# Graph network, first loop: products of message scalars and edge directions on VectorE, one instruction a step, in place of 24 on ScalarE

## The chip, the cores and the metric

The kernel runs on one core of one Trainium2 chip. The metric is the device time of one execution in microseconds (us); a version's time is the median of its runs. The engines are TensorE (PE; its weight loads are shown apart as PEld), VectorE (DVE), ScalarE (ACT), GpSimd (POOL) and SyncE (SP). They run side by side and wait for one another by semaphores only.

## What is computed

Two layers of a graph network over 6250 nodes with 128 features and 106250 directed edges sorted by their target. Only the first is touched. Its edge part, cut to what matters:

```python
Y1 = SQ3 * edge_vec / |edge_vec|                 # 3 numbers per edge
w = (silu(silu(emb @ w0 + b0) @ w1 + b1) @ w2 + b2).reshape(-1, 4, 32)
ss, vv = xs[senders], xv[senders]                # 32 scalars, 32 x 3 vectors of the source node
m0 = w[:, 0] * ss
m1 = w[:, 1][:, :, None] * ss[:, :, None] * Y1[:, None, :]
m2 = w[:, 2][:, :, None] * vv
m3 = w[:, 3] * (einsum('emc,ec->em', vv, Y1) / SQ3)
msg = segment_sum over receivers of (m0, m3), (m1, m2)
```

The node part behind it (two small products, a residual, a layer norm) and the second layer, with its own loop over the edges, stay as they are. The change is about `m1`.

## The kernel before

The edges lie in tiles of 128 (edges on the partitions). A step of the first loop takes 8 tiles; there are 104 steps, written as 26 iterations of 4 steps (`SLOTS`), most of them in hardware loops. `edges0` writes one program for each engine. A step, numbered j, uses one of two sets of buffers (h = j % 2) and one of four buffers for gathered rows (u = j % 4). By engine, in the order of its program:

- **GpSimd** issues 8 indirect DMAs a step (`gather_step`, L731), each fetching 128 node rows into `gx`. Ahead of a step's gathers it waits for the list of indices (L744), for `used` (L746: the buffer was read) and, from iteration 17 on, for TensorE's second MLP product, `h2_mm` (L749), which paces it.
- **SyncE** loads the list of indices for the next iteration (L888) once the gathers of this slot have landed, and `emb` (L892) once TensorE has done its first product `h1_mm`; both stand in one queue, with the loads and stores of the node part between them.
- **TensorE** keeps the MLP three steps ahead. In step j: 8 products of the one-hot matrix with the first half of the message columns into `ps_a` (L1105, waits for `half_ok`), the third MLP product, which makes the weights of step j + 1 in `ps_w` (L785, L787, signals `w_mm`), the second MLP product (L197, waits for `h1_ok`, signals `h2_mm`), 8 products with the other half of the columns (L1105, waits for `plain_ok` and `y_ok`, signals `sum_mm`), and the first MLP product for a later step (L1101, waits for `h2_ok`, signals `h1_mm`). Products of the node part (L1111, L1117, L1118, L1130) stand between these.
- **VectorE** makes the message columns: L808 `vy` = vectors times directions; L805 `ws` = weights times scalars (waits for `w_mm`, signals `ws_ok`); L811 and L814 the first half (`m0`, `m2`; signals `half_ok`); L818, L818, L821 the dot product and `m3` (signals `plain_ok`); between them L1259 adds the sums of the step before from `ps_a` to the node sums at a start position that is read into a register (L1255, TENSOR_LOAD). L1250 makes the next one-hot matrix. A part of the node work follows in each step.
- **ScalarE** does the silu of the first and of the second product (L192), and makes `m1` = `ws` times direction in `by_component` (L829): for each of the 8 tiles and each of the 3 components one activation of 128 x 32 with the direction as its scale for each partition, 24 a step, 12 ahead of the first silu and 12 behind it, then `y_ok`. Copies of the node part (L1018, L1023, L1033, L1039) and, once an iteration, two table loads (L1063, L1066) stand between.

`ws`, `y`, `vy`, `gx` and `msg` lie in SBUF, `ps_w` and `ps_a` in PSUM. The last steps are unrolled; there VectorE makes `m1` itself, by `all_components` (L824), since they are handled in parts.

Of the kernel before, what the change touches and what calls it, by code (L numbers as in the profile page):

```python
# [31 lines left out]
TPS = 8  # L32
PPS = TPS // 2
SLOTS = 4
# [26 lines left out]
LOOPS = STEPS // SLOTS  # L61
# [783 lines left out]
def edges0(nc, a, k, dram, w, later, v, mlp, left):  # L845

    with ExitStack() as ctx:
# [12 lines left out]
        gate = gate_x = k["gate"]  # L860
        used, half_ok, plain_ok, ws_ok, y_ok, own, sum_mm, acc_own = (
            m.sem(n) for n in ("used", "half_ok", "plain_ok", "ws_ok", "y_ok", "own0", "sum_mm", "acc_own"))
        later_ld, iota_ok, w_ok, w_own, sums_ok = (m.sem(n) for n in ("later_ld", "iota_ok", "w_ok", "w_own0",
# [19 lines left out]
        with nc.Block(no_gpsimd_drain=True) as block:  # L883
# [115 lines left out]
            def _(e):  # L999
                def components(j, h, tiles):  # L1000
                    for t in tiles:
                        last = msgs[h].by_component(e, t, w["y"][:, bass.ds(j * TPS + t, 1), :]
                                                    .rearrange("p t c -> p (t c)"))
                    return last

                CLEAR = (T * NACC - v["end"]) // (LAG * SLOTS)
# [34 lines left out]
                def steps(i, unit, before, last=False):  # L1041
                    for u in range(SLOTS):
                        j, h = i * SLOTS + u, u % 2
                        if not last or u < SLOTS - 2:
                            e.wait_ge(ws_ok, j + 1)
                            components(j, h, range(0, TPS // 2))
                            layer0_silu(e, w, mlp, 1, j + 3)
                            components(j, h, range(TPS // 2, TPS)).then_inc(y_ok, 1)
                        if before and u == 0:
                            table_out(i - (LAG + 1), 1)  # L1050
                        if unit and u == 2:
                            nodes_t(i - LAG)
                        if unit and u == 3 and not last:
                            table_out(i - LAG, 0)
                        if not last or u < SLOTS - 2:
                            layer0_silu(e, w, mlp, 2, j + 3)
                        if not unit:
                            clear_high(j)
                        if unit and u == 0:
                            copy_sums(i - LAG, i * SLOTS)  # L1060
                        if unit and u == 1:
                            clear_sums(i - LAG)
                            e.preload_act_table(ACT.Sqrt)  # L1063
                            root(i - (LAG - 1), slice(0, UB))
                            if not last:
                                e.preload_act_table(ACT.Silu)  # L1066
# [31 lines left out]
            def _(e):  # L1098
# [68 lines left out]
                def steps(i, unit, before, last=False):  # L1167
                    for u in range(SLOTS - 1 if last else SLOTS):
# [19 lines left out]
                        e.wait_ge(plain_ok, j + 2)  # L1188
                        if not last or u < SLOTS - 2:
                            e.wait_ge(y_ok, j + 1)  # L1190
                        sums(h, 1).then_inc(sum_mm, 1)
# [54 lines left out]
            def _(e):  # L1246
# [124 lines left out]

                def messages(i, u, first=False, unit=False, before=False, whole=False, counted=False):

# [9 lines left out]
                    mine.w2_product(e, wt, vec).then_inc(half_ok, 1)  # L1383
                    if whole:
                        e.wait_ge(ws_ok, j + 1)
                        mine.all_components(e, y)
                    e.wait_ge(own, j * 3 + 1)
# [57 lines left out]
                for u in range(SLOTS - 1):  # L1445
                    messages(LOOPS - 1, u, unit=True, before=True, whole=u == SLOTS - 2)
                last_first(0)
# [1148 lines left out]
```

## Time and profile before

| | us |
|---|---|
| median of 3 runs | 2890.57 (2885.65 to 2907.28) |
| profiled execution, its own time | 2876.12 |
| span of the profiled execution | 2874.2 |
| busy in the span: PE / DVE | 2014.0 / 1473.3 |
| busy in the span: ACT / POOL | 1329.9 / 1601.4 |
| ScalarE's L829, 2448 instructions | 539.8 |

The profile is of one execution. An instruction's row has its start, its duration, engine, line, what it writes and reads, and in brackets the idle time of its engine just before it with what ended that. "issue" is idle time that nothing in the profile ended; "remote" is a releaser that the profile does not name. DVE starts an instruction while the one before still writes, so that starts lie closer than durations. The first loop lies between about 60 and 1494 us.

### The profile page before, as it was taken

Reading aid. Unit: us, or ns where it says so; the run is one execution under the profiler, and the core shown is the slowest. Engines: PE = TensorE matmul, PEld = TensorE weight load, DVE = VectorE, ACT = ScalarE, POOL = GpSimd, SP = SyncE. Lnnn points to the kernel's source line nnn. Section 1 sums busy time; section 2 is a strip of 40 time slices with the busy share of each in tenths; the row PEclk is TensorE's granted clock in tenths of the full one; section 3 lists DMA queues with packets and bytes.
Section 4 is the critical chain, followed back from the end, with each engine's and each line's share of the span. In section 5 each row is a group of like instructions: output and inputs, shape, how many; then the busy total and the mean of one; then the engine's idle time right before and its main releaser. Section 6 shows DMA issues by size and latency. Waiting matters only on the chain. (4 is left out here: it accounts for less than half of the span.)

```text
span 2874.2 us, 43625 instructions
## 1 busy us (share of the span) xinstructions
PE 2014.0 (70%) x10027; PEld 1570.4 (55%) x10027; DVE 1473.3 (51%) x3718; ACT 1329.9 (46%) x4378; POOL 1601.4 (56%) x1680
## 2 busy tenths in 40 slices
PE   6777678768777787878785766565666566566656
PEld 4555455545554565656563655554665555555555
DVE  6443344334343444444453445665666666666666
ACT  5545456445464565555542333434343334334333
POOL 6655454555544555656546555566666666665662
PEclk7778788878787888889897787787777767767778
DMA  8311112111121121222125553333333333333331
GB/s 266 91 38 45 49 53 63 55 54 49 50 63 50 53 59 57 60 60 65 52 81 164 154 143 88 96 94 91 91 97 94 93 91 92 97 85 95 94 94 49
DMA packets 221613, 238.23 MB, mean 83 GB/s; under 512 B 73212, under 2 KB 163240, under 8 KB 221131
## 3 DMA queue, kind: packets, MB, share of 16 engines
q0 software_dynamic: 53472, 110.50, 14.8%
q1 hardware_dynamic: 79835, 71.35, 8.1%
q10 hardware_dynamic: 88256, 55.83, 7.4%
q8 instruction: 16, 0.26, 0.0%
q14 instruction: 34, 0.28, 0.0%
HBM read 191.88 MB, written 45.62 MB: 83 GB/s over the span
## 5 line engine op out<-in xcount | busy, mean ns | idle before, releaser
L731 POOL DMA_INDIRECT gx<-node_d,idx x815 | 789.2, 968 | 647.8 <-issue 279.1
L731 POOL DMA_INDIRECT gp<-p_tab_d,idx x831 | 789.0, 949 | 555.8 <-issue 272.1
L1105 PEld LDWEIGHTS ps_a<-hot,msg 128*128 128x128 f32 x3324 | 469.4, 220 | 315.8 <-issue 294.2
L1105 PE MATMUL ps_a<-hot,msg 128*128 128x128 f32 x3324 | 506.0, 310 | 153.9 <-issue 80.4
L829 ACT ACTIVATE msg<-ws,y 128x32 f32<-128x32 f32 x2448 | 539.8, 310 | 5.6 <-issue 3.1
L2140 PE MATMUL ps_e<-win,hot_x 128*128 128x129 f32 x1664 | 328.9, 365 | 289.3 <-issue 181.8
L2140 PEld LDWEIGHTS ps_e<-win,hot_x 128*128 128x128 f32 x1664 | 298.6, 271 | 314.7 <-issue 211.0
L805 DVE TENSOR_TENSOR ws<-ps_w,gx 128x256 f32<-128x256 f32 (+1 forms) x105 | 44.2, 421 | 521.6 <-remote 386.5
L192 ACT ACTIVATE h<-ps_h,b 128x512 f32<-128x512 f32 x208 | 141.8, 682 | 332.8 <-remote 198.0
L2277 DVE TENSOR_TENSOR hot_x<-key_row,ps_s 128x1024 f32<-128x1024 bf16 x104 | 126.4, 1216 | 323.7 <-remote 299.4
L2025 ACT ACTIVATE hid<-hid,score 128x128 f32<-128x128 f32 x832 | 277.5, 392 | 10.1
L2229 PE MATMUL ps_g<-hot,hid 128*128 128x128 f32 x1664 | 237.8, 294 | 43.1 <-issue 41.6
L2229 PEld LDWEIGHTS ps_g<-hot,hid 128*128 128x128 f32 x1664 | 228.3, 209 | 60.4 <-issue 51.4
L787 PE MATMUL ps_w<-w,h 128*128 128x256 f32 x832 | 246.2, 444 | 11.0 <-issue 10.7
L787 PEld LDWEIGHTS ps_w<-w,h 128*128 128x128 f32 x832 | 172.1, 217 | 90.6 <-issue 67.0
L2021 ACT ACTIVATE score<-hid 128x3 f32<-128x3 f32 (+1 forms) x312 | 60.6, 194 | 272.9 <-DVE hid L2322 181.7
L2322 DVE TENSOR_TENSOR hid<-ps_e,gp 128x387 f32<-128x387 f32 (+1 forms) x312 | 142.0, 509 | 73.8 <-remote 66.2
L1259 DVE TENSOR_TENSOR acc<-acc,ps_a 128x256 f32 x105 | 44.3, 422 | 264.3 <-remote 189.1
L1101 PE MATMUL ps_h<-emb,w 16*128 16x512 f32 x202 | 136.8, 762 | 38.9 <-ACT h L192 29.5
L2299 DVE TENSOR_TENSOR acc<-acc,ps_g 128x128 f32 x416 | 119.4, 287 | 25.8 <-issue 12.1
L2235 PE MATMUL ps_s<-hot_n,sc 128*128 128x128 f32 x416 | 76.4, 310 | 79.2 <-issue 59.6
L1039 ACT ACTIVATE acc<-ps_x 128x258 f32<-128x258 f32 x44 | 16.9, 384 | 247.0 <-remote 196.9
(304 smaller groups left out, 2556.7 us busy)
## 6 DMA issues: line engine op xcount, KB each, us to landing
win<-q_tab_d ACTq DMA_DIRECT2D x408, 64.5 KB
key_row<-key_row_d ACTq DMA_DIRECT2D x100, 256.0 KB
gp<-p_tab_d,idx POOLq DMA_INDIRECT x831
gx<-node_d,idx POOLq DMA_INDIRECT x815
p_tab_d<-acc SPq DMA_DIRECT2D x23, 516.0 KB
q_tab_d<-unit_area SPq DMA_DIRECT2D x36, 258.0 KB
q_tab_d<-acc SPq DMA_DIRECT2D x5, 774.0 KB, 4.0
emb<-emb_d SPq DMA_DIRECT2D x102, 32.0 KB
```

The lines of the kernel that those rows point to most:

```text
L192: e.activation(mlp[f"h{layer}"][:], mlp["ps_h"][:], ACT.Silu, bias=w[f"b{layer - 1}"][:]).then_inc(ok, 1)
L731: e.indirect_dma_start(out=buf[:, h, t, :], out_offset=None, in_=table, in_offset=bass.IndirectOffsetOnAxis(ap=idx[:, h, t:t + 1], axis=0) ...
L787: last = e.matmul(ps_w[:, 2 * t:2 * t + 2, :], h2[:, t * P:(t + 1) * P], w["w2"][:], start=False, stop=t % 2 == 1)
L829: last = e.activation(self.cols[1][:, tile, c, :], self.ws[:, tile, :], ACT.Copy, scale=y[:, c:c + 1])
L1101: e.matmul(ps_h[:], w["w0"][:], emb[:, h, :], start=True, stop=True).then_inc(h1_mm, 1)
L1105: last = e.matmul(ps_a[:, h, b, :], msgs[h].tile(t, b), hot[:, h, t, :], start=t == tiles.start, stop=t == tiles.stop - 1)
L2025: last = e.activation(hid[:, h, t, 0:H], hid[:, h, t, 0:H], ACT.Relu, scale=score[:, h, t:t + 1])
L2140: last = e.matmul(ps_e[:, q, at:at + PW], hot_x[:, h, t, :], win[:, h, t // 2, :], start=True, stop=True)
L2229: e.matmul(ps_g[:, h, t // 2, :], hid[:, h, t, 0:H], hot[:, h, t, :], start=t % 2 == 0, stop=t % 2 == 1)
L2277: e.tensor_tensor(hot_x[:, h].rearrange("p t n -> p (t n)"), key_row[:, h, :], part.to_broadcast([P, TPS * P]), ALU.is_equal).then_inc(hx_ ...
L2299: e.tensor_tensor(at, at, ps_g[:, h, p, :].rearrange("p (t n) -> p t n", t=T), ALU.add)\
L2322: e.tensor_tensor(hid[:, h, mine, :], ps_e[:, q, 0:n * PW].rearrange("p (t n) -> p t n", t=n), gp[:, u, mine, :], ALU.add).then_inc(pre_ok, 1)
```

## The change

The 24 activations a step go away, with the semaphore `y_ok` and TensorE's wait for it. VectorE calls `all_components` in every step, between the first half of the columns and the dot product: one product of `ws` (repeated over 3 components) with `y` (repeated over 32 columns), 128 x 768, both operands in SBUF. It waits for VectorE's own `ws_ok`.

```diff
@@ block.scalar
-                def components(j, h, tiles):
-                    for t in tiles:
-                        last = msgs[h].by_component(e, t, w["y"][:, bass.ds(j * TPS + t, 1), :]
-                                                    .rearrange("p t c -> p (t c)"))
-                    return last
...
                         if not last or u < SLOTS - 2:
-                            e.wait_ge(ws_ok, j + 1)
-                            components(j, h, range(0, TPS // 2))
                             layer0_silu(e, w, mlp, 1, j + 3)
-                            components(j, h, range(TPS // 2, TPS)).then_inc(y_ok, 1)
@@ block.tensor
                         e.wait_ge(plain_ok, j + 2)
-                        if not last or u < SLOTS - 2:
-                            e.wait_ge(y_ok, j + 1)
                         sums(h, 1).then_inc(sum_mm, 1)
@@ block.vector, messages
                     mine.w2_product(e, wt, vec).then_inc(half_ok, 1)
-                    if whole:
-                        e.wait_ge(ws_ok, j + 1)
-                        mine.all_components(e, y)
+                    e.wait_ge(ws_ok, j + 1)
+                    mine.all_components(e, y)
                     e.wait_ge(own, j * 3 + 1)
                     mine.dot_sum(e, 1).then_inc(own, 1)
```

How the order on the engines changes. Line numbers of the changed kernel are lower by 9 on TensorE's L1105 (now L1096), by 6 on ScalarE's copies and by 11 on VectorE's lines from L1250 on.

VectorE, one step in the looped part, before:

```order
L808 TENSOR_TENSOR vy<-gx,y 128x768 [waits landed0]
L805 TENSOR_TENSOR ws<-ps_w,gx 128x256 [waits w_mm]
L811 TENSOR_TENSOR msg<-ps_w,gx 128x8x32
L814 TENSOR_TENSOR msg<-ps_w,gx 128x8x96
L818 TENSOR_TENSOR vy<-vy 128x8x32 [waits own0]
L1255 TENSOR_LOAD start [waits half_ok]
L1259 ISA [waits acc_own,sum_mm]
L1259 TENSOR_TENSOR acc<-acc,ps_a 128x2x128
```

and now:

```order
L808 TENSOR_TENSOR vy<-gx,y 128x768 [waits landed0]
L805 TENSOR_TENSOR ws<-ps_w,gx 128x256 [waits w_mm]
L811 TENSOR_TENSOR msg<-ps_w,gx 128x8x32
L814 TENSOR_TENSOR msg<-ps_w,gx 128x8x96
L824 TENSOR_TENSOR msg<-ws,y 128x8x96 [waits ws_ok]
L818 TENSOR_TENSOR vy<-vy 128x8x32 [waits own0]
L1244 TENSOR_LOAD start [waits half_ok]
L1248 ISA [waits acc_own,sum_mm]
L1248 TENSOR_TENSOR acc<-acc,ps_a 128x2x128
```

L824 has come between L814 and L818; the rest keeps its order, and the register load still waits for `half_ok` alone.

ScalarE, a step of an iteration that has the table loads behind it, before:

```order
L829 ACTIVATE msg<-ws,y 128x32 [waits ws_ok]
L829 ACTIVATE msg<-ws,y 128x32 x11
L192 ACTIVATE h<-ps_h,b 128x512 [waits h1_mm]
L829 ACTIVATE msg<-ws,y 128x32 x12
L192 ACTIVATE h<-ps_h,b 128x512 [waits h2_mm]
L1023 ACTIVATE acc<-zero 128x2x256 [waits sums_ok0]
L1063 ACT_TABLE_LOAD
L1028 ACTIVATE rstd<-rstd 128x2 [waits var_ok_0]
```

and now:

```order
L192 ACTIVATE h<-ps_h,b 128x512 [waits h1_mm]
L192 ACTIVATE h<-ps_h,b 128x512 [waits h2_mm]
L1017 ACTIVATE acc<-zero 128x2x256 [waits sums_ok0]
L1054 ACT_TABLE_LOAD
L1022 ACTIVATE rstd<-rstd 128x2 [waits var_ok_0]
```

Both silus and the copies stay in their order; the wait for `ws_ok` has left this engine.

TensorE, end of a step, before:

```order
L197 MATMUL ps_h<-h,w 128x512 [waits h1_ok]
L1105 MATMUL ps_a<-hot,msg 128x128 [waits y_ok,plain_ok]
L1105 MATMUL ps_a<-hot,msg 128x128 x7
L1101 MATMUL ps_h<-emb,w 128x512 [waits emb_in0,h2_ok]
L1105 MATMUL ps_a<-hot,msg 128x128 [waits acc_own,half_ok]
```

and now:

```order
L197 MATMUL ps_h<-h,w 128x512 [waits h1_ok]
L1096 MATMUL ps_a<-hot,msg 128x128 [waits plain_ok]
L1096 MATMUL ps_a<-hot,msg 128x128 x7
L1092 MATMUL ps_h<-emb,w 128x512 [waits emb_in0,h2_ok]
L1096 MATMUL ps_a<-hot,msg 128x128 [waits acc_own,half_ok]
```

Nothing moves here; one of two waits is gone.

## Rows read from the trace of the kernel before

**Rows 1.** busy us by stretch: start:end, length, PE, PEld, DVE, ACT, POOL, PE clock
```profile
60.00:1016.00 956.00, 719.97 (x3302) 503.79 (x3303) 400.03 (x790) 499.98 (x1838) 491.36 (x509) 0.80 0.19 55
1016.00:1494.00 478.00, 396.23 (x1900) 282.86 (x1899) 216.63 (x446) 274.84 (x1012) 274.94 (x287) 0.87 0.21 62
```

**Rows 2.** groups by line, 60 to 1494 us; busy, mean ns, idle before
```profile
L731 POOL DMA_INDIRECT gx<-node_d,idx x793 | 765.1, 965 | 639.6 <-issue 272.7 <-DMA idx<-in_src 209.1 <-PE ps_h L197 77.5
...
L829 ACT ACTIVATE msg<-ws,y 128x32 f32<-128x32 f32 x2448 | 539.8, 310 | 5.6 <-issue 3.1 <-DVE ws L805 2.2
...
L805 DVE TENSOR_TENSOR ws<-ps_w,gx 128x256 f32<-128x256 f32 (+1 forms) x105 | 44.2, 421 | 521.6 <-remote 386.5 <-PE ps_w L787 97.5 <-issue 37.5
...
L1259 DVE TENSOR_TENSOR acc<-acc,ps_a 128x256 f32 x103 | 43.5, 422 | 263.8 <-remote 189.1 <-PE ps_a L1105 38.2 <-issue 36.5
```

**Rows 3.** waits of GpSimd, 60 to 1016 us; total, times, longest
```profile
POOL gx L731 <- DMA idx<-in_src: 209.1, 29, 12.4
```

**Rows 4.** waits of GpSimd, 1016 to 1494 us
```profile
POOL gx L731 <- PE ps_h L197: 77.5, 13, 18.9
POOL gx L731 <- remote: 50.7, 20, 2.7
```

**Rows 5.** waits of TensorE, 60 to 1494 us
```profile
PE ps_a L1105 <- remote: 41.1, 11, 8.3
...
PE ps_a L1105 <- ACT msg L829: 21.6, 17, 2.4
```

**Rows 6.** order of time, one step about 1178 us: start, duration, engine, line
```profile
1178.43 1.99 PE L787 MATMUL ps_w<-w,h 128*128 128x256 f32 x8
...
1180.34 2.64 ACT L829 ACTIVATE msg<-ws,y 128x32 f32<-128x32 f32 x12
...
1182.69 0.94 POOL L731 DMA_INDIRECT gx<-node_d,idx  x1 [0.30 <-issue]
...
1185.44 3.16 PE L1105 MATMUL ps_a<-hot,msg 128*128 128x128 f32 x16 [3.82 <-remote]
1185.49 0.42 DVE L805 TENSOR_TENSOR ws<-ps_w,gx 128x256 f32<-128x256 f32 x1 [6.50 <-remote]
1185.63 0.38 ACT L1033 ACTIVATE acc<-ps_x 128x256 f32<-128x256 f32 x1 [2.65 <-remote]
...
1195.09 0.94 POOL L731 DMA_INDIRECT gx<-node_d,idx  x1 [0.30 <-issue]
...
1195.67 1.02 PE L197 MATMUL ps_h<-h,w 128*128 128x512 f32 x2
...
1197.88 0.42 DVE L805 TENSOR_TENSOR ws<-ps_w,gx 128x256 f32<-128x256 f32 x1 [5.56 <-remote]
...
1198.72 0.94 POOL L731 DMA_INDIRECT gx<-node_d,idx  x1 [2.70 <-PE ps_h L197]
```

**Rows 7.** order of time, VectorE without the whole product at 1198 us
```profile
1198.55 0.95 DVE L814 TENSOR_TENSOR msg<-ps_w,gx 128x768 f32<-128x768 f32 x1
...
1200.35 0.42 DVE L1259 TENSOR_TENSOR acc<-acc,ps_a 128x256 f32 x1 [0.52 <-issue]
```

**Rows 8.** order of time, VectorE with it, second last step
```profile
1484.09 0.95 DVE L814 TENSOR_TENSOR msg<-ps_w,gx 128x768 f32<-128x768 f32 x1
...
1484.95 0.95 DVE L824 TENSOR_TENSOR msg<-ws,y 128x768 f32<-128x768 f32 x1
...
1486.15 0.41 DVE L1259 TENSOR_TENSOR acc<-acc,ps_a 128x256 f32 x1
```

**Rows 9.** order of time, a gather that starts beside L808
```profile
1085.24 0.95 DVE L808 TENSOR_TENSOR vy<-gx,y 128x768 f32<-128x768 f32 x1
1085.37 1.64 POOL L731 DMA_INDIRECT gx<-node_d,idx  x1 [0.30 <-issue]
```

**Rows 10.** TensorE waits for L829, first of six
```profile
365.99 1.24 PE L1105 MATMUL ps_a<-hot,msg 128*128 128x128 f32 x9 [1.16 <-ACT msg L829]
```

**Rows 11.** TensorE waits for L829, last of the six
```profile
946.46 1.80 PE L1105 MATMUL ps_a<-hot,msg 128*128 128x128 f32 x14 [0.67 <-ACT msg L829]
```

More of the change, by code:

```diff
@@ L860, in edges0 @@
         gate = gate_x = k["gate"]
-        used, half_ok, plain_ok, ws_ok, y_ok, own, sum_mm, acc_own = (
-            m.sem(n) for n in ("used", "half_ok", "plain_ok", "ws_ok", "y_ok", "own0", "sum_mm", "acc_own"))
+        used, half_ok, plain_ok, ws_ok, own, sum_mm, acc_own = (
+            m.sem(n) for n in ("used", "half_ok", "plain_ok", "ws_ok", "own0", "sum_mm", "acc_own"))
         later_ld, iota_ok, w_ok, w_own, sums_ok = (m.sem(n) for n in ("later_ld", "iota_ok", "w_ok", "w_own0",
@@ L1042, in steps @@
                     for u in range(SLOTS):
-                        j, h = i * SLOTS + u, u % 2
+                        j = i * SLOTS + u
                         if not last or u < SLOTS - 2:
-                            e.wait_ge(ws_ok, j + 1)
-                            components(j, h, range(0, TPS // 2))
                             layer0_silu(e, w, mlp, 1, j + 3)
-                            components(j, h, range(TPS // 2, TPS)).then_inc(y_ok, 1)
                         if before and u == 0:
@@ L1370, in last_second, with messages @@
                     mine.w3_product(e, wt).then_inc(plain_ok, 1)
-                def messages(i, u, first=False, unit=False, before=False, whole=False, counted=False):
+                def messages(i, u, first=False, unit=False, before=False, counted=False):
                     j, h = i * SLOTS + u, u % 2
@@ L1445, in _ @@
                 for u in range(SLOTS - 1):
-                    messages(LOOPS - 1, u, unit=True, before=True, whole=u == SLOTS - 2)
+                    messages(LOOPS - 1, u, unit=True, before=True)
                 last_first(0)
```

## The prediction

> **What bounds the kernel now.** I looked first at busy time by stretch. In the first loop (60 to 1494 us, 104 steps) no engine is full: TensorE 720 of 956 us and then 396 of 478, ScalarE 500 and 275, VectorE 400 and 217, GpSimd 491 and 275 [rows 1]. The loop is held by waits between engines. Then I read the groups by line. VectorE stands idle 521.6 us before L805, so it is the least loaded of the engines in the chain; ScalarE's L829 takes 539.8 us in 2448 instructions and has almost no idle time before it [rows 2]. That looks like a bound, but who waits for it? TensorE is stopped at L1105 by L829 for 21.6 us in 17 waits, and for 41.1 us in 11 waits with an unnamed releaser [rows 5], 62.7 us together. That is the largest sum that taking L829 away can set free directly.
>
> Next the waits of GpSimd, which issues eight gathers a step. To 1016 us it waits 209.1 us in 29 waits for lists of indices [rows 3]; SyncE loads them behind a wait for TensorE's first MLP product. After 1016 us it waits for the second MLP product, 77.5 us in 13 and 50.7 us in 20 waits [rows 4]. Busy and waiting together fill the loop on this engine.
>
> The order of time shows why. TensorE's last weight product (L787) ends at 1178.43 + 1.99 = 1180.42, and VectorE, idle, starts L805 only at 1185.49. The last gather of the batch ends at 1182.69 + 0.94 = 1183.63. The same happens a step later: the batch's last gather ends at 1195.09 + 0.94 = 1196.03, VectorE starts at 1197.88, and the second product, over at 1195.67 + 1.02 = 1196.69, lets GpSimd go on at 1198.72 [rows 6]. So what is signalled in the later part of a batch of gathers reaches the others about 1.85 us after its last gather. From one L805 at 1185.49 to the next at 1197.88 is one period: 12.39 us, of which 9.70 are eight gathers of 0.95 with 0.30 between them, 1.85 this delay, and 0.84 GpSimd's start behind the signal (1198.72 - 1197.88). In the second stretch this period, not ScalarE's work, sets most steps.
>
> **The change part by part.** ScalarE loses L829: 539.8 us of its 774.8 in the loop. Only the start of its other work moves, and TensorE loses the wait for y_ok.
>
> (a) *The waits of TensorE.* Of the 17 short waits, six lie where GpSimd has no batch running: the first ends at 365.99 and cost 1.16 us, the last at 946.46 with 0.67 [rows 10, 11]; the others cost 0.25, 1.87, 1.22 and 1.51, all six 6.7 us. There TensorE's progress is what GpSimd's next indices wait for, so I count them in full: -6.7. The others fall in a batch, whose end is not TensorE's to move: 0, with a bound of 21.6 - 6.7 = 14.9 us of gain.
>
> (b) *The waits of the second kind.* In the second stretch one step in four has one like that of 3.82 us at 1185.44: ScalarE ended L829 at 1180.34 + 2.64 = 1182.98, within the batch, and TensorE saw it after the batch [rows 6]. Without it these 16 products run at once. But TensorE's next work waits for ScalarE's copy, which is released only after the batch and ends at 1185.63 + 0.38 = 1186.01, where these products now end at 1188.60; so TensorE gains at most 2.6 us, not 3.8, and some 2.4 with the start of a matmul. Its second product would end at 1194.3 in place of 1196.69; GpSimd still sees it about 1.7 to 1.85 us after 1196.03, near 1197.8 in place of 1197.9 or so. The gain is 0.2 us in each of 9 iterations: -1.8. Bounds: 0, and -41.1 if all of it comes back.
>
> (c) *VectorE's new instruction.* L824 already stands in the second last step: 0.95 us, and the next instruction starts 0.86 after it. Over 102 steps that is 88 us of VectorE's time. How much lies on its chain? Without it, L814 starts at 1198.55 and the sum L1259 at 1200.35, after 0.52 us of idle time that nobody released [rows 7]: the engine is reading the start position into a register there. With it, L814 starts at 1484.09 and L1259 at 1486.15 [rows 8]. That is 2.06 in place of 1.80 us: the new instruction fills the gap and costs 0.26 us, not 0.86. All 36.5 us of such idle time before L1259 [rows 2] are cover. What is queued behind L824 is the dot product, the sum and L821; TensorE needs L821's result only behind a third and a second product, 1.99 and 1.02 us [rows 6]. The first half of the message columns (L814, half_ok) goes ahead of L824 and isn't late. With 521.6 us idle before L805 I cost this 0. If the cover is gone (steps where L805 follows L808 at once), it costs 0.26 to 0.86 us each; the upper bound is 88 us.
>
> (d) *GpSimd beside it.* A gather takes 0.95 us, but one that starts 0.13 us after L808 took 1.64 and so ended at 1087.01, where L808 ended at 1086.19 [rows 9]: 0.69 us longer. L808 reads both operands from SBUF. L814 reads one from PSUM, and the gather that starts at 1198.72, 0.17 us after it, takes 0.94 [rows 6, 7]. L824 reads both from SBUF. The Trainium skill says so too (SBUF — State Buffer, "Who interferes with whom"): a VectorE instruction with two SBUF inputs contends with a GpSimd instruction that reads SBUF, and the later one waits. The same section infers that such a product does not hold up the making of descriptors; by that this part would cost nothing, by the row it costs, and the row decides.
> Size: 793 gathers at 965 ns [rows 2] against 950 are 11.9 us too much. The operations with two SBUF inputs are now L808 (0.95) and two L818 (0.84 us) a step, 183 us in 102 steps, so 0.065 us of delay per us, and 0.062 us for one L824. But in the second stretch the two are in step. GpSimd's first gather starts 0.84 us after L805, its second 0.95 + 0.30 later, at 2.09 [rows 6]. L824 would start 1.53 and end 2.48 us after L805's start (1197.88 to 1198.55 is 0.67 [rows 6, 7], then 0.86 [rows 8]). The second gather starts inside it and waits for its end, less the 0.13 us that the pair of rows 9 leaves uncounted (0.82 to the end, 0.69 of delay): 0.26 us. About 27 of the 36 steps there have this order (rows 4 count 33 waits, a few of them much longer): 27 x 0.26 = +7.0. The other 66 steps at 0.062: +4.1. Bounds: 0, and 0.69 x 102 = 70 us.
>
> **Sum.** -6.7 - 1.8 + 0 + 7.0 + 4.1 = +2.6 us. The profiled execution took 2876.1 us (span 2874.2), so 2879; it lies 14.5 us below the median of 2890.6, so the forecast for a median is 2893 us. A measurement of this kernel can tell about 1%, 29 us, from no change; this is no change.
>
> **The rivals.**
> *TensorE's waits come back whole.* For it: 62.7 us are really waited, ScalarE is freed of 540 us, and TensorE is the busiest engine. Against: in batches the partners' releases come after the last gather anyway. Then -62.7 + 11.1 = -52, 2839 us.
> *The second product gets through before the batch ends.* If TensorE, ahead by some us, signals in the early part of a batch, GpSimd runs on without the 1.7 us: 27 x 1.7 = 46 us less. Against: the weight product that ended at 1180.42 did so 3.2 us before the batch's end and still came 5 us late [rows 6], and the gain of 2.4 us is small beside a batch of 9.7. -46 - 8.5 + 11.1 = -43, 2847 us.
> *The gathers are lengthened in every step* (the slower side). Place: the gather that starts beside L824, on the engine whose period sets the step. If each step meets it with about 0.5 us, between the 0.26 worked out and the 0.69 seen, it is +51 - 8.5 = +43, 2933 us. From (28.9 + 8.5) / 102 = 0.37 us a step on it is slower by over 1%. For it: both engines are released by the same signal, so they meet systematically. Against: VectorE is released when GpSimd pauses, and in the first stretch that pause for indices is 7.2 us on average (209.1 / 29), so that L824 is over before the gathers begin.
> *VectorE becomes the bound*: +88 us, 2978. Against: 521.6 us idle.
> That the change doesn't do what it says I rule out: in its order every ScalarE product is gone and L824 stands once in each step.
>
> **How the numbers follow.** Forecast's case 0.52, the first rival 0.17, the second 0.08, the third 0.18, the fourth 0.05. Faster by over 1%: 0.25; within 1%: 0.52; slower: 0.23. The steps of this loop are irregular, and any shift regroups batches; the likeliest case's own range is 2868 to 2915. With the rivals I give 2845 to 2930, which leaves out the fourth and the far ends of the first and third.
>
> **What would show it.** Right: ScalarE's busy time falls by some 540 us and VectorE's rises by some 90, while the loop still ends near 1494 us; GpSimd's waits in the second stretch keep their 2.5 us; L731's mean rises from 965 to about 980 ns, with second gathers of 1.2 us; idle time before L1259 by "issue" nearly vanishes. Wrong: TensorE's idle time in the loop falls by 50 us and the span with it (first rival); periods of GpSimd under 12 us (second); L731 near 1000 ns or more and a longer loop (third); idle time before L805 gone (fourth).

## The result and the profile after

The changed kernel took 2803.18 us (median of 4 runs, 2793.11 to 2817.75), the kernel before 2888.11 us beside it. The ratio is 0.9695, 95% interval [0.9639, 0.9751]: faster by 3%. The forecast was 2893 us with a range of 2845 to 2930. Two later comparisons gave 0.9815 [0.9742, 0.9888] and 0.9735 [0.9688, 0.9781].

One thing must be known to read the numbers: the experiments came to several chips, and these are of two kinds. On some the kernel before takes 2868 to 2922 us, as in the first comparison; on two others it takes 2162 and 2164 us. They are called slower and quicker chips here; two of the slower ones were used twice and were slow both times. Ratios are always to the kernel before on the same chip.

The head of the page of the changed kernel, profiled at 2817.75 us (the slowest of its four runs):

```profile
span 2815.9 us, 38846 instructions
PE 1998.1 (71%) x10027; PEld 1548.5 (55%) x10027; DVE 1563.1 (56%) x3820; ACT 818.1 (29%) x1930; POOL 1632.6 (58%) x1680
```

The span is 58.3 us shorter (before 2874.2). ScalarE is busy 511.8 us less (L829 alone was 539.8; what is left in the loop takes 263.9 in place of 235.0), VectorE 89.8 more; GpSimd, whose program nobody touched, 31.2 more. The groups of the first loop, 60 to 1494 us, against [rows 2]:

```profile
L731 POOL DMA_INDIRECT gx<-node_d,idx x792 | 796.7, 1006 | 549.6 <-issue 238.8 <-DMA idx<-in_src 173.1 <-PE ps_h L197 80.8
...
L824 DVE TENSOR_TENSOR msg<-ws,y 128x768 f32<-128x768 f32 (+1 forms) x105 | 98.9, 942 | 0.0
L1248 DVE TENSOR_TENSOR acc<-acc,ps_a 128x256 f32 x105 | 44.1, 420 | 288.0 <-remote 240.0 <-PE ps_a L1096 26.3 <-issue 20.8
L805 DVE TENSOR_TENSOR ws<-ps_w,gx 128x256 f32<-128x256 f32 (+1 forms) x105 | 44.1, 420 | 340.6 <-remote 232.6 <-PE ps_w L787 71.4 <-issue 36.5
```

The last gather of the loop ends at 1414.2 us, before at 1482.3: the loop is 68 us shorter, and the rest of the program 10 us longer. Most of the gain shows at L731. Its gathers take 31.6 us more (796.7 against 765.1, mean 1006 ns in place of 965), and its idle time is 90.0 us less (549.6 against 639.6), together -58.4. So GpSimd waits less. The busy time by stretch, split where the pacing begins (963.5 us; before 1015.6), for [rows 1]:

```profile
60.00:964.00 904.00, 711.77 (x3306) 495.68 (x3305) 457.34 (x857) 168.75 (x256) 508.20 (x508) 0.81 0.22 58
964.00:1426.00 462.00, 396.04 (x1916) 277.86 (x1915) 248.76 (x491) 95.12 (x148) 289.64 (x287) 0.87 0.24 64
```

The first stretch is 52 us shorter, the second 16. The granted clock of TensorE is 0.81 and 0.87 in place of 0.80 and 0.87, so the clock is not where the time went. GpSimd's waits in the two stretches, for [rows 3, 4]:

```profile
POOL gx L731 <- DMA idx<-in_src: 173.1, 25, 10.5
...
POOL gx L731 <- PE ps_h L197: 80.8, 15, 26.8
POOL gx L731 <- remote: 23.2, 10, 3.1
```

For indices it waits 173.1 us in 25 waits, before 209.1 in 29. Another 33.9 us of the difference is idle time shown as "issue" (238.8 against 272.7), whose cause the profile doesn't name. Of the short waits with an unnamed releaser, the ones of some 2.5 us at each paced batch, 10 are left of 20. The order of time shows such a wait, and one that did not come:

```profile
1182.00 0.95 POOL L731 DMA_INDIRECT gx<-node_d,idx  x1 [2.51 <-remote]
...
1182.70 0.95 DVE L824 TENSOR_TENSOR msg<-ws,y 128x768 f32<-128x768 f32 x1
1183.26 1.21 POOL L731 DMA_INDIRECT gx<-node_d,idx  x1 [0.30 <-issue]
...
1187.53 1.99 PE L787 MATMUL ps_w<-w,h 128*128 128x256 f32 x8
...
1189.56 0.42 DVE L805 TENSOR_TENSOR ws<-ps_w,gx 128x256 f32<-128x256 f32 x1 [2.12 <-PE ps_w L787]
...
1190.21 1.02 PE L197 MATMUL ps_h<-h,w 128*128 128x512 f32 x2
...
1191.07 0.94 POOL L731 DMA_INDIRECT gx<-node_d,idx  x1 [0.30 <-issue]
...
1192.74 0.95 POOL L731 DMA_INDIRECT gx<-node_d,idx  x1 [0.73 <-PE ps_h L197]
```

The batch that begins at 1182.00 waited 2.51 us. The next one, at 1192.74, waited 0.73: the second MLP product was over at 1191.23, before the last gather's end (1192.01), and GpSimd went on without the 1.85 us. In the same batch the weight product ended at 1189.52, 7.5 us in, and VectorE started on it at 1189.56, where the one of the prediction came 5 us late.

Counted over the trace, such cases are what changed. GpSimd is idle for over 0.5 us before a gather 81 times in the loop of the kernel before and 61 times now; more batches run into one another. Of the weight products that end 5 to 8 us into an unbroken run of gathers while VectorE stands idle, 35 of 36 reached VectorE over 0.6 us late before, 14 of 28 now. The rows also show the contention as forecast: L824 starts inside the first gather, the second gather (1183.26) is held up by it and takes 1.21 us in place of 0.95, the 0.26 us of the prediction to the digit.

### The profile page after: what moved, and what is told of

Its sections match the earlier page's. It is cut to its first block and busy times, and to the rows that moved or that the text cites. A ratio compares the mean times of both kernels' runs of the same rounds, so it can differ in the third digit from the quotient of the medians.

```text
span 2815.9 us, 38846 instructions
## 1 busy us (share of the span) xinstructions
PE 1998.1 (71%) x10027; PEld 1548.5 (55%) x10027; DVE 1563.1 (56%) x3820; ACT 818.1 (29%) x1930; POOL 1632.6 (58%) x1680
## 5 line engine op out<-in xcount | busy, mean ns | idle before, releaser
L731 POOL DMA_INDIRECT gx<-node_d,idx x815 | 821.8, 1008 | 557.2 <-issue 245.5
L731 POOL DMA_INDIRECT gp<-p_tab_d,idx x831 | 787.8, 948 | 567.4 <-issue 281.8
L1096 PEld LDWEIGHTS ps_a<-hot,msg 128*128 128x128 f32 x3324 | 457.2, 214 | 205.7 <-issue 189.9
L1096 PE MATMUL ps_a<-hot,msg 128*128 128x128 f32 x3324 | 485.0, 302 | 52.2 <-issue 43.6
L2128 PE MATMUL ps_e<-win,hot_x 128*128 128x129 f32 x1664 | 319.8, 359 | 253.7 <-issue 163.3
L2128 PEld LDWEIGHTS ps_e<-win,hot_x 128*128 128x128 f32 x1664 | 289.1, 264 | 285.3 <-issue 199.5
L787 PE MATMUL ps_w<-w,h 128*128 128x256 f32 x832 | 254.9, 446 | 28.8 <-issue 27.7
L805 DVE TENSOR_TENSOR ws<-ps_w,gx 128x256 f32<-128x256 f32 (+1 forms) x105 | 44.1, 420 | 340.6 <-remote 232.6
L1248 DVE TENSOR_TENSOR acc<-acc,ps_a 128x256 f32 x105 | 44.1, 420 | 288.0 <-remote 240.0
L1092 PE MATMUL ps_h<-emb,w 16*128 16x512 f32 x202 | 129.6, 725 | 62.9 <-ACT h L192 58.4
L197 PE MATMUL ps_h<-h,w 128*128 128x512 f32 x208 | 127.7, 700 | 21.9 <-ACT h L192 21.1
L2273 DVE TENSOR_TENSOR hot<-ps_s,key 128x1024 f32<-128x1024 f32 x104 | 126.4, 1216 | 2.7 <-issue 2.7
```

Source lines behind the costliest of these rows:

```text
L197: e.matmul(mlp["ps_h"][:], w["w1"][:], mlp["h1"][:], start=True, stop=True).then_inc(mlp["h2_mm"], 1)
L731: e.indirect_dma_start(out=buf[:, h, t, :], out_offset=None, in_=table, in_offset=bass.IndirectOffsetOnAxis(ap=idx[:, h, t:t + 1], axis=0) ...
L787: last = e.matmul(ps_w[:, 2 * t:2 * t + 2, :], h2[:, t * P:(t + 1) * P], w["w2"][:], start=False, stop=t % 2 == 1)
L1092: e.matmul(ps_h[:], w["w0"][:], emb[:, h, :], start=True, stop=True).then_inc(h1_mm, 1)
L1096: last = e.matmul(ps_a[:, h, b, :], msgs[h].tile(t, b), hot[:, h, t, :], start=t == tiles.start, stop=t == tiles.stop - 1)
L2128: last = e.matmul(ps_e[:, q, at:at + PW], hot_x[:, h, t, :], win[:, h, t // 2, :], start=True, stop=True)
```

## The experiments

The theories at the start: theory 1, TensorE's removed wait for `y_ok` brings the gain; theory 2, ScalarE's freed time does. Beside them stood the price of VectorE's product. All ratios are to the kernel before in the same comparison:

| run | ScalarE's 24 | wait for y | slower chips | quicker chips |
|---|---|---|---|---|
| changed kernel | no | no | 0.9695, 0.9815, 0.9735 | not run |
| wait | no | yes | 0.9755 | 1.0031, 1.0063 |
| load | yes | no | 0.9984 | 1.0033 |
| both | yes | yes | 0.9981 | 1.0035, 1.0070 |
| wspsum | no | no | 0.9766 | 1.0003, 1.0000 |
| loadhalf | 12 | no | 0.9854 | not run |
| loadfew | 10, longer | no | 0.9899 | not run |
| loadahead | yes, all ahead of the silus | no | 0.9941 | not run |
| silufirst (kernel before, other order) | yes | yes | 0.9992 | 1.0004 |

**The first four, on a quicker chip.** The run load is the changed kernel with this on ScalarE (all edits in short form):

```diff
+    def scaled(j, tiles):   # 128 x 32 each
+        for t in tiles:
+            for c in range(3):
+                last = e.activation(scratch[:, t, c, :], zero[:, 0:MUL], Copy, scale=y[:, c:c + 1])
...
+    e.wait_ge(ws_ok, j + 1)
+    scaled(j, range(0, TPS // 2))
     layer0_silu(e, w, mlp, 1, j + 3)
+    scaled(j, range(TPS // 2, TPS))
```

> The changed kernel, and ScalarE still runs 24 activations of 128 x 32 a step (12 ahead of the first silu, 12 behind it, behind its wait for ws_ok), but reads zeros and writes a scratch buffer that nobody reads; TensorE waits for nothing of it. The output stays that of the reference. Theory 1 (TensorE's removed wait for y_ok brings the gain, since a microsecond early in a batch of gathers decides whether the next batch's condition gets through): 2803 us as the changed kernel, ratio 0.97 to the kernel before. Theory 2 (ScalarE's freed time brings it, its silus no longer stand behind activations): 2888 us or more, ratio 1.0. If both share in it, the time lies between and says how much each has.

Measured: 2171.19 us, 1.0033 [1.0023, 1.0044]. The run wait, without the load:

```diff
+    e.wait_ge(ws_ok, j + 1)                 # ScalarE
     layer0_silu(e, w, mlp, 1, j + 3)
+    e.sem_inc(y_ok, 1)
...
+    e.wait_ge(y_ok, j + 1)                  # TensorE
     sums(h, 1).then_inc(sum_mm, 1)
```

> The changed kernel with the wait but without the load: ScalarE waits for ws_ok ahead of its first silu and then signals y_ok, with no activations, and TensorE waits for y_ok ahead of its second 8 products. Theory 1 (the wait of TensorE): most of the gain is gone, 2860 to 2888 us, less than the whole since the signal now comes some 5 us earlier than behind 24 activations. Theory 2 (ScalarE's load): 2803 us, ratio 0.97.

Measured: 2170.38 us, 1.0031 [1.0021, 1.0042]. With both edits together:

> The changed kernel with the wait and the load: 24 activations into the scratch buffer as in the run load, y_ok behind them and TensorE's wait for it. Against the kernel before only VectorE's additional product (and what it holds up on GpSimd) is left, so this prices it. My contention term: gathers at 1000 ns and more instead of 965, 2888 + 30 to 40 = 2920 to 2930 us. If the gathers' lengthening is absorbed in their waits: 2888 to 2900. Less than 2888 would say that the product on VectorE brings a gain by itself, which no theory of mine explains.

Measured: 2171.34 us, 1.0035 [1.0023, 1.0046]. And the contention alone:

```diff
-    mine.ws_product(e, wt, s).then_inc(ws_ok, 1)          # ws <- ps_w * gx, in SBUF
+    e.tensor_tensor(wt[:, :, 1, :], wt[:, :, 1, :], s, ALU.mult).then_inc(ws_ok, 1)   # in PSUM
...
-    mine.all_components(e, y)                             # L824 from ws in SBUF
+    mine.all_from(e, wt[:, :, 1, :], y)                   # the same from PSUM
```

> The changed kernel, with ws (weights times scalars, L805) written over its own weights in PSUM instead of into SBUF, so that the new product L824 has one operand in PSUM, one in SBUF, at the same size and place. If two SBUF operands are what makes a gather wait for the end of L824, the gathers' mean falls from 1008 to about 980 ns (21 us less over the first loop), and the time to 2780 to 2795 us if gather time counts in full. If any VectorE product holds a gather up, or the gathers' lengthening isn't on the path: 2803 us, or, with L805 or L824 slower by their PSUM access, a little more.

Measured: 2163.50 us, 1.0003 [0.9993, 1.0013]. The kernel before took 2162.3 us there, 726 us less than in the first comparison. GpSimd's waits in the run both, 60 to 1076 us, say why the theories could not be told apart:

```profile
POOL gx L731 <- issue: 246.6, 779, 9.5
POOL gx L731 <- PE ps_h L197: 1.8, 6, 0.3
POOL gx L731 <- DVEq L1391: 1.2, 4, 0.3
POOL gx L731 <- DMA idx<-in_src: 0.3, 1, 0.3
```

Nothing but the 0.3 us between gathers is left: here the loop is GpSimd's own work, and no partner's signal comes late. So what counts is the length of the gathers. The group of all gathers of the first layer, in both and then in wspsum:

```profile
L731 POOL DMA_INDIRECT gx<-node_d,idx x815 | 792.7, 973 | 257.6 <-issue 254.2 <-PE ps_h L197 1.8 <-DVEq L1391 1.2
```

```profile
L731 POOL DMA_INDIRECT gx<-node_d,idx x815 | 785.7, 964 | 257.0 <-issue 255.1 <-PE ps_h L197 0.9 <-DMA idx<-in_src 0.6
```

7.0 us less, and the medians differ by 7.8 (2171.34 - 2163.50). The run wspsum also has neither load nor wait, but load and wait, which lack one of the two each, are as slow as both (2171.19 and 2170.38). The runs on the other quicker chip say the same with larger numbers: wait2, both2 and wspsum2 have gathers of 801.5, 802.7 and 787.6 us and medians of 2177.36, 2178.88 and 2163.08. On such a chip the contention counts about in full, and an operand in PSUM removes it. One instance in both:

```profile
617.19 0.95 DVE L824 TENSOR_TENSOR msg<-ws,y 128x768 f32<-128x768 f32 x1
...
617.60 1.35 POOL L731 DMA_INDIRECT gx<-node_d,idx  x1 [0.30 <-issue]
```

**On a slower chip: the changed kernel again, and the load.**

> The changed kernel as it is, once more. In the first four runs the kernel before took 2162 us, not 2888, and its variants had no waits of GpSimd above 0.3 us and no late signals, so those runs say nothing on where 85 us went in the first comparison. If this run again has a kernel before of about 2162 us: with ratio 1.003 both theories' parts (TensorE's wait, ScalarE's load) are worth nothing there, and only the product on VectorE costs (run both: 1.0035). If it has one of about 2888 us: ratio 0.97, as in the first comparison.

Measured: 2859.71 us, 0.9815 [0.9742, 0.9888], the kernel before 2920.81.

> The changed kernel with ScalarE's 24 activations a step into a scratch buffer, TensorE not waiting for them, once more. With a kernel before of about 2162 us: 1.003, as before. With one of about 2888 us: by theory 1 (TensorE's removed wait) 0.97 as the changed kernel, by theory 2 (ScalarE's load) 1.0.

Measured: 2913.83 us, 0.9984 [0.9943, 1.0025]. With ScalarE's load back and TensorE not waiting for it, the whole gain is gone. Theory 1 falls. The counts go back too: GpSimd is idle for over 0.5 us 77 times, in changed2 67 times, and of the weight products late in a run 34 of 37 are held up, in changed2 18 of 29.

**Four more, which came to a quicker chip.**

> The run wait once more (ScalarE waits for ws_ok and signals y_ok without activations, TensorE waits for y_ok), for a chip state in which the kernel before takes about 2890 us. The run load2 there stood at 0.998 to the kernel before, with ScalarE's 24 activations alone, so theory 2 (ScalarE's load) leads. Theory 2: ratio 0.97 to 0.985 as the changed kernel. Theory 1 (TensorE's wait and the coupling through ScalarE): 0.99 to 1.0. If the kernel before takes about 2162 us: 1.003.

Measured: 2177.36 us, 1.0063 [1.0047, 1.0078].

> The run both once more (activations, y_ok and TensorE's wait, all back; only VectorE's product is added to the kernel before). With a kernel before of about 2890 us: by my contention term, gathers near 1000 ns instead of 965 and the time counted in full, 1.010 to 1.015; if the wait is worth nothing beside the load, as load2 says, the same as load2, 0.998; by theory 1 it must lie above load2 by most of the 62.7 us, 1.02. With one of about 2162 us: 1.0035.

Measured: 2178.88 us, 1.0070 [1.0057, 1.0083].

```diff
-    e.wait_ge(ws_ok, j + 1)
-    components(j, h, range(0, TPS // 2))
     layer0_silu(e, w, mlp, 1, j + 3)
-    components(j, h, range(TPS // 2, TPS)).then_inc(y_ok, 1)
+    e.wait_ge(ws_ok, j + 1)
+    components(j, h, range(0, TPS)).then_inc(y_ok, 1)
```

> The kernel before with one order changed: ScalarE does the first silu ahead of all 24 activations (and ahead of its wait for ws_ok) instead of between two halves of 12; y_ok comes one silu later relative to the first half. VectorE has no additional product. If what a silu queued behind activations costs is the point (theory 2), part of the gain comes without moving any work: 0.98 to 0.99 with a kernel before of about 2890 us. If only the removed work or the wait for y_ok counts: 1.00 or a little above.

Measured: 2164.84 us, 1.0004 [0.9995, 1.0014].

> The run wspsum once more (ws in PSUM, so that L824 has one operand there). In the first call it was 0.0032 below its siblings, with gathers no longer lengthened by L824. With a kernel before of about 2890 us and the changed kernel at 0.97 to 0.98: if lengthened gathers count in full, some 20 us less, 0.965 to 0.975; if they are absorbed by waits of GpSimd, as the changed kernel.

Measured: 2163.08 us, 1.0000 [0.9991, 1.0009]. The four repeat the price of VectorE's product, 0.3 to 0.7%, and its removal; on the theories they are silent.

**On a slower chip: the wait, and ws in PSUM.**

> The run wait a third time (ScalarE waits for ws_ok and signals y_ok without activations, TensorE waits for y_ok). With a kernel before of about 2890 us, theory 2 (ScalarE's load) gives 0.97 to 0.985 as the changed kernel, theory 1 (TensorE's wait and the coupling through ScalarE) 0.99 to 1.0. With one of about 2162 us: 1.003 to 1.006, as twice before.

Measured: 2848.75 us, 0.9755 [0.9701, 0.9808]. The whole gain is there with TensorE's wait and the coupling through ScalarE in place. Theory 2 holds as far as it says that ScalarE's load makes the difference; by which path, these two runs don't say.

> The run wspsum a third time (ws in PSUM). With a kernel before of about 2890 us: 0.965 to 0.975 if lengthened gathers count in full, 0.98 as the changed kernel if GpSimd's waits absorb them. With one of about 2162 us: 1.000, as twice before.

Measured: 2853.05 us, 0.9766 [0.9708, 0.9824], no better than the changed kernel. Its gathers (60 to 1494 us), and those of changed2:

```profile
L731 POOL DMA_INDIRECT gx<-node_d,idx x793 | 774.6, 977 | 603.9 <-issue 274.6 <-DMA idx<-in_src 188.7 <-PE ps_h L197 73.6
```

```profile
L731 POOL DMA_INDIRECT gx<-node_d,idx x795 | 794.5, 999 | 580.3 <-issue 263.6 <-DMA idx<-in_src 187.5 <-PE ps_h L197 77.6
```

The gathers are 19.9 us shorter and the idle time 23.6 us longer (the two ran on different slower chips; beside wspsum3 stood wait3, 0.9755). Here the partners set the pace and GpSimd's waits absorb what the gathers gain or lose.

**Which part of the load? Its place, its time, its number of instructions.** The order of silufirst on a slower chip:

> The kernel before with ScalarE's first silu ahead of all 24 activations, once more, for a kernel before near 2900 us. ScalarE's load is now shown to be what counts there (load2 0.998, wait3 0.976). If what costs is the first silu behind 12 activations: 0.98 to 0.99. If it is the second silu, which now stands behind 24 instead of 12, or the load as a whole: 1.00 to 1.01. With a kernel before near 2164 us: 1.000 as before.

Measured: 2914.43 us, 0.9992 [0.9957, 1.0027]. The first silu's place is worth nothing. Then ten long activations in place of 24 short ones:

```diff
+    for c in range(5):      # ahead of the first silu, and once more behind it
+        last = e.activation(scratch[:, c], zero[:], Copy, scale=y[:, c % 3:c % 3 + 1])   # 128 x 512
```

Ahead of each five activations ScalarE also waits for the end of the five before, which no other variant does.

> The changed kernel with about the same busy time on ScalarE as in load2 but in 10 instructions a step instead of 24: five activations of 128 x 512 (zeros into a scratch buffer) ahead of the first silu and five behind it, TensorE not waiting for them. If the time that the silus stand queued is what costs (busy time): as load2, 0.998. If the number of instructions, their fetching or their dispatch is: nearer to the changed kernel, 0.98. With a kernel before near 2164 us: 1.003 to 1.007.

Measured: 2891.62 us, 0.9899 [0.9860, 0.9938]. The group on ScalarE in loadfew, and the one in load2:

```profile
L1007 ACT ACTIVATE scratch<-zero,y 128x512 bf16<-128x512 f32 x1020 | 645.2, 711 | 5.0 <-DVE ws L805 2.6 <-issue 2.1
```

```profile
L1005 ACT ACTIVATE scratch<-zero,y 128x32 f32<-128x32 f32 x2448 | 543.3, 313 | 5.2 <-issue 3.9 <-DVE ws L805 0.8
```

102 us more of busy time, and yet less lost than in load2 on the same chip, whose interval begins just where this one ends. Busy time isn't the measure. All 24 ahead of the first silu, none between the silus:

```diff
+    scaled(j, range(0, TPS))
     layer0_silu(e, w, mlp, 1, j + 3)
```

> The changed kernel with all 24 activations (zeros into a scratch buffer) ahead of the first silu and none between it and the second; TensorE doesn't wait for them. The traces so far, from the end of a product into ps_h to the start of its silu, summed over the loop: second silu 315 us in the kernel before, 338 in load2, 333 in silufirst2 (ratios 1.000, 0.998, 0.999); 265 in loadfew (0.990), 254 and 264 in changed2 and wait3 (0.9815, 0.9755); the first silu shows no such order (204, 256, 84, 337, 240, 233). If the second silu's lateness is what costs, this run is near the changed kernel, 0.975 to 0.985, with ScalarE's load complete. If the load's number of instructions or its time is, wherever it stands: 0.998. With a kernel before near 2164 us: 1.003 to 1.007.

Measured: 2860.40 us, 0.9941 [0.9899, 0.9983]: at most a small part of the gain. In its trace the second silus start some 235 us in sum behind their products, about as in the kernels with the gain (254 in changed2) and not as in load2 (338): the lateness is gone and the gain with it, so the second silu's lateness does not explain it.

> The run both a third time (activations, y_ok and TensorE's wait are back; only VectorE's product is added to the kernel before). With a kernel before near 2900 us: 1.00 if the lengthened gathers are absorbed by GpSimd's waits, as wspsum3 against the changed kernel says; 1.010 to 1.015 by my contention term. With one near 2164 us: 1.0035 to 1.007.

Measured: 2863.66 us, 0.9981 [0.9946, 1.0017]. VectorE's product costs nothing that can be told on a slower chip, and the wait for y adds nothing to the load that can be told (load2 0.9984); both within about 0.4%, some 10 us. Last, half the load and the changed kernel beside it:

```diff
+    scaled(j, range(0, TPS // 4))
     layer0_silu(e, w, mlp, 1, j + 3)
+    scaled(j, range(TPS // 4, TPS // 2))
```

> The changed kernel with half of ScalarE's load: 12 activations a step into a scratch buffer, 6 ahead of the first silu and 6 behind it, TensorE not waiting. With a kernel before near 2900 us, by theory 2 with a share for each instruction taken away: half-way, 0.985 to 0.99. If the load costs only from some fill on: as the changed kernel, 0.975. With one near 2164 us: 1.003 to 1.007.

Measured: 2879.43 us, 0.9854 [0.9803, 0.9905].

> The changed kernel a third time, beside loadhalf on the same chip. With a kernel before near 2900 us: 0.97 to 0.98. With one near 2164 us, where it has not run yet: 1.003 to 1.007, as load, wait and both there, which have in common with it only VectorE's product.

Measured: 2840.32 us, 0.9735 [0.9688, 0.9781]. Half the load costs about half of the gain; with this one point between, no threshold shows.

The heads of the pages hold the number that goes with the ratios. In load2, loadhalf, loadfew and wait3, in this order:

```profile
span 2905.4 us, 43625 instructions
```

```profile
span 2864.2 us, 41249 instructions
```

```profile
span 2876.3 us, 40577 instructions
```

```profile
span 2854.0 us, 39083 instructions
```

The ratios are 0.9984, 0.9854, 0.9899 and 0.9755, and 38846 instructions in the changed kernel go with 0.9735. The kernel before has 43625, 4779 more, though only 2448 activations went: beside them ScalarE's program held 2304 register instructions at L829, nearly one for each, which went too and came back with the load. On the line from 1 to 0.9735, 41249 instructions give 0.987 and 39083 give 0.975, both within their intervals; 40577 give 0.983, below the 0.986 at which loadfew's begins, and loadahead with 43625 should stand at 1 and its interval ends at 0.9983. So the number is closer than the busy time, but it misses two of five variants; time and place have a part. It was not varied alone, and that it is the cause is not shown.

## Why the prediction was wrong

**What bounds the kernel.** That the loop is held by waits was right for the slower chips. That signals sent in the later part of a batch arrive behind it was right as a description of the kernel before (35 of 36 late), but I took it for fixed, and in the changed kernel only half of them are late. On the quicker chips GpSimd waits for none.

**Steps (a) and (b), TensorE's wait for y_ok, -6.7 and -1.8 us.** That they are small was right: with the load in place the wait is worth 0.9984 against 0.9981, without it wait3 (0.9755) lies among the changed kernel's ratios. These runs can't tell 8.5 us from nothing. The first rival, in which the 62.7 us come back, gave the time nearest to the result, and its sign came too: TensorE's idle time in the loop fell by 60 us (258 in place of 318) and the span by 58. Its reason is refuted all the same, since the wait itself is worth nothing that can be told.

**The step that failed** stands ahead of them: "ScalarE loses L829: 539.8 us of its 774.8 in the loop. Only the start of its other work moves, and TensorE loses the wait for y_ok." I priced the removal of 2448 activations by who waits for their result, and put the removal itself at nothing, with no bound. The runs put the whole gain there: load2 against changed2 in one comparison is 2913.83 against 2859.71 us, 54 us, and half the load cost about half (0.9854 between 0.9735 and 0.998). By what path the removed activations, with their register instructions, let signals through stays open.

**The second rival**, in which the second product gets through before the batch ends, saw the form that the gain takes in the second stretch: 10 of 20 such waits are gone, and at 1192.74 one is 0.73 us long. But that stretch gave 16 us, and the first, where GpSimd waits for indices and for which I had no such rival, gave 52. The argument under (a) that a wait in a batch is worth 0, because the batch's end stands fixed, was too narrow: a signal can be seen within the batch, and where batches end moves (81 idle times before, 61 after).

**(c) VectorE's product, 0.** Right within 0.4% on the slower chips: both3 0.9981. The idle time "issue" before L1248 fell from 36.5 to 20.8 us and did not vanish, so that sign was too strong.

**(d) Gathers beside L824, +11.1.** The place and the 0.26 us of one pair were right. The sum was too small. L731 took 31.6 us more, at 1006 ns and not 980, but not all of that is L824's: without it the same gathers take 765.1 us in the trace before and 776.7 in silufirst2, with its operand in PSUM 774.6 (wspsum3), and 788 to 797 in the runs that have it from SBUF. Some 20 us is L824's share, about twice the 11.1. Yet no effect of it on the time can be told there (wspsum3), since the waits of GpSimd absorb it. That was the error of adding it to the sum: I had shown that GpSimd idles 639.6 us, and still counted its longer instructions as path. On the quicker chips, where it doesn't idle, the term counts: 7.0 us of gather time and 7.8 us of time on one, 15.1 and 15.8 on the other (both2 against wspsum2). The Trainium skill (SBUF — State Buffer, "Who interferes with whom") says that a VectorE instruction with two SBUF inputs contends with GpSimd's reads, and one with at most one such input does not; wspsum against both agrees (964 against 973 ns). The inference from the same section that the prediction gives, by which such a product doesn't hold up the making of descriptors, doesn't hold here: the gather at 617.60 took 1.35 us.

**The third rival**, slower: its mechanism was real, its price of 0.5 us a step was not paid on the slower chips. On the quicker ones it decides the sign, 1.0031 to 1.0070 in every variant that has L824 from SBUF. The fourth fell: VectorE still idles 340.6 us before L805, though 181 us less than before.

## What to carry to other kernels

When many small instructions go away, bound the effect of the instructions themselves and not only the waits for their result; a variant that puts the load back into a scratch buffer, with nobody waiting, prices it in one run. A delay on an engine that idles between batches belongs into the sum only if its own work sets the pace, and this can differ from chip to chip: here the same change is 3% faster on one kind of chip and, by its siblings, 0.3 to 0.7% slower on the other. Keeping one operand of the moved product in PSUM (wspsum) is nowhere slower than the kernel before beyond the interval: 0.9766 on the slower, 1.0003 and 1.0000 on the quicker chips. An estimate of a delay that rests on a pattern in the trace before holds only as long as the change leaves the pattern in place.

## What the hardware showed that I had not expected

**Two kinds of chips.** The same kernel takes 2888 and 2162 us. On the slower kind GpSimd idles 639.6 us before the loop's gathers [rows 2], on the quicker 257.6 (run both), of which nearly all is the 0.3 us between gathers. The difference, 726 us, over 43625 instructions is 16.6 ns for each; what the removal of 4779 instructions brought in the first comparison, 84.9 us, is 17.8 ns for each. That looks like one cost for every instruction on the slower chips, but the agreement is in part chance. The other two comparisons of the changed kernel give 12.8 and 16.8 ns. By stage, before against silufirst (the same instructions in another order), the slower chip needs 18.6 ns more for each instruction up to the last gather of the first loop and 14.0 for each one behind it. And wspsum3 against wspsum, with some 4800 instructions fewer in the loop, still loses 375 us there, where before against silufirst loses 408: 21.8 ns each.

What takes longer is not the instructions themselves: VectorE is busy 1473.3 us on the slower and 1477.8 on the quicker chip, ScalarE 1329.9 and 1329.4, GpSimd 1601.4 and 1600.7. TensorE alone differs, 2014.0 and 1764.3, with a granted clock of 0.795 and 0.906 over the span. Whether the lower clock is a cause of the waiting or comes from it, no run here shows. The Trainium skill (NOTIFIC — the notification-queue block, "7.1 Overflow: three behaviours, one of which stalls the engine") states that the path on which engines report their instructions holds its producers back rather than lose a record; no run here shows whether that, the supply of instructions, the clock or something else is it.

**TensorE runs dry late in a long batch.** On a slower chip, here in the changed kernel, the products of one sum, which elsewhere follow each other at once (16 in 1.95 us), come singly, with idle time that nothing in the profile releases, while GpSimd is deep in 16 gathers:

```profile
980.34 0.61 PE L1096 MATMUL ps_a<-hot,msg 128*128 128x128 f32 x4
...
981.27 0.27 PE L1096 MATMUL ps_a<-hot,msg 128*128 128x128 f32 x1 [0.32 <-issue]
...
982.00 0.27 PE L1096 MATMUL ps_a<-hot,msg 128*128 128x128 f32 x1 [0.46 <-issue]
...
983.41 0.27 PE L1096 MATMUL ps_a<-hot,msg 128*128 128x128 f32 x1 [1.15 <-issue]
...
986.95 1.45 PE L1096 MATMUL ps_a<-hot,msg 128*128 128x128 f32 x6 [0.94 <-issue]
```

No semaphore stands between these. So on the slower chips it is not only signals that are late while gathers are issued, but instructions themselves. The group of these products in the first loop, in the kernel before, in the changed kernel and, on a quicker chip, in both:

```profile
L1105 PE MATMUL ps_a<-hot,msg 128*128 128x128 f32 x3300 | 502.9, 310 | 153.9 <-issue 80.4 <-remote 41.1 <-ACT msg L829 21.6
```

```profile
L1096 PE MATMUL ps_a<-hot,msg 128*128 128x128 f32 x3324 | 485.0, 302 | 52.2 <-issue 43.6 <-DVE msg L814 7.9
```

```profile
L1107 PE MATMUL ps_a<-hot,msg 128*128 128x128 f32 x3324 | 431.7, 285 | 63.8 <-DVE msg L814 49.0 <-ACT scratch L1005 12.1 <-issue 1.9
```

Idle time by "issue" is 80.4 us before, 43.6 after, 1.9 on the quicker chip. It too goes with ScalarE's load in the runs of one chip: 68.4 us in load2, 37.3 in changed2. In both3 it is 23.0, beside 42.7 of waits for named and unnamed partners, so it is no measure by itself.
